# The down projection as one level of Strassen: seven half-size products, their sums on VectorE, weights streamed from DRAM

## The reference, cut to what matters

```python
x = fwht(x * SU_ug) / SCALE
x_up = x @ W_up.T * (Wscale_ug[:INTER] * SCALE)
x_gate = x @ W_gate.T * (Wscale_ug[INTER:] * SCALE)
x = jax.nn.silu(x_gate) * x_up
x = fwht(x * SU_dp) / SCALE
x = x @ W_down.T * (Wscale_dp * SCALE)
```

## Time and profile before

| | us |
|---|---|
| median of 3 runs | 1850.89 (1848.28 to 1851.36) |
| the profiled execution, device time | 1849.29 |
| its span | 1847.2 |
| main work begins on PE | 161.9 |
| block 1 begins on PE | 268.3 |
| last matmul ends | 1841.9 |
| one block, 1 to 14 | 104.9 |

### The profile page before, as it was taken

One profiled execution on the slowest core, in us unless ns is written; L12 is line 12 of the kernel. 1 busy time (PEld: TensorE's weight loads), 2 busy tenths in 40 slices (PEclk: granted clock), 3 DMA queues, 4 the chain that ended last, 5 costly groups with the idle time before them and its releaser, 6 DMA issues.

```text
span 1847.2 us, 37874 instructions
## 1 busy us (share of the span) xinstructions
PE 1794.1 (97%) x13746; PEld 1241.8 (67%) x13746; DVE 1383.8 (75%) x2859; ACT 1224.6 (66%) x2582; POOL 307.7 (17%) x270
## 2 busy tenths in 40 slices
PE   4878999999999999999999999999999999999998
PEld 2336667576766768676766758677666757676675
DVE  6987867869586877858586877958686776958686
ACT  7967848576574848566584847666584857667483
POOL 0000212213030212203021221203021220303021
PEclk9999999999999999999999999999999999999999
DMA  8221223121312223131312322131322213131232
GB/s 326 69 69 49 56 58 81 32 82 38 81 47 62 77 47 76 41 78 41 89 47 58 81 45 76 36 77 47 86 53 58 81 34 75 43 81 47 65 75 58
DMA packets 217573, 125.68 MB, mean 68 GB/s; under 512 B 179662, under 2 KB 180790, under 8 KB 216886
## 3 DMA queue, kind: packets, MB, share of 16 engines
q1 hardware_dynamic: 216870, 122.30, 25.1%
q10 hardware_dynamic: 528, 1.05, 0.2%
HBM read 72.18 MB, written 8.65 MB: 44 GB/s over the span
## 4 chain that ended last, share of the span: by engine, by line
PE 90%; DVE 5%; ACT 1%; DMA 1%; issue 1%; SPq 1%; DVEq 1%; ACTq 0%
PE bank L912 88%; DVE wug L624 1%; DVE wi L666 1%; DMA wi<-n_L_attn_out_proj_w_dram 1%; PE bank L728 1%; PE bank L729 0%; DVE big L509 0%; ACT big L460 0%; DVE wo L675 0%; ACT wi L432 0%; SPq L873 0%; PE bank L717 0%; DVE wd L509 0%; DVE big L510 0%; ACT wi L464 0%
## 5 line engine op out<-in xcount | busy, mean ns | idle before, releaser
L912 PE MATMUL bank<-pair,wug 128*128 128x256 f16 x6144 | 699.8, 273 | 0.0
L912 PEld LDWEIGHTS bank<-pair,wug 128*128 128x128 f16 x6144 | 596.2, 98 | 90.4 <-issue 3.4
L912 PE MATMUL bank<-wd,h 128*128 128x512 f16 x1536 | 360.3, 379 | 0.0
L1185 POOL TENSOR_TENSOR state<-state,dec 128x512 f32<-128x512 f32 x64 | 87.5, 1377 | 1066.3 <-ACT neg L1100 805.7
L912 PEld LDWEIGHTS bank<-wd,h 128*128 128x128 f16 x1536 | 149.2, 98 | 160.4 <-DVE h L1243 0.2
L1232 DVE SCALAR_TENSOR_TENSOR pair<-pair,conv 128x256 f32<-128x256 f32 x384 | 180.2, 514 | 79.0 <-ACT pair L1048 69.1
L912 PE MATMUL bank<-wi,pair 128*128 128x512 f16 (+1 forms) x1152 | 201.6, 330 | 3.1 <-DVEq L1345 3.1
L912 PE MATMUL bank<-pair,wi 128*128 128x256 f16 x1536 | 173.1, 273 | 0.0
L912 PEld LDWEIGHTS bank<-wi,pair 128*128 128x128 f16 x1152 | 101.4, 99 | 98.1 <-issue 3.9
L1114 ACT ACTIVATE Mx<-Mx,cs_own 128x128 f32<-128x128 f32 x512 | 162.2, 388 | 7.6 <-DMA Mx<-cs_rows 7.4
L912 PEld LDWEIGHTS bank<-pair,wi 128*128 128x128 f16 x1536 | 150.0, 98 | 17.0
(11 more groups left out here) (253 smaller groups left out, 2717.0 us busy)
## 6 DMA issues: line engine op xcount, KB each, us to landing
Mx<-cs_rows SPq DMA_DIRECT2D x128, 256.0 KB, 3.6
pair<-in_L_attn_u_dram SPq DMA_DIRECT2D x17, 512.0 KB, 3.6
Mx<-in_L_attn_u_dram SPq DMA_DIRECT2D x16, 512.0 KB, 3.7
out_dram<-Mx SPq DMA_DIRECT2D x16, 512.0 KB, 2.8
big<-in_L_ffn_W_down_dram SPq DMA_DIRECT2D x2, 2048.0 KB, 17.8
wug<-in_L_attn_in_proj_w_dram SPq DMA_DIRECT2D x2, 2048.0 KB, 13.4
pair<-in_L_ffn_W_gate_dram SPq DMA_DIRECT2D x4, 1024.0 KB, 5.3
pair<-in_L_ffn_W_up_dram SPq DMA_DIRECT2D x3, 1024.0 KB, 16.6
```

Source lines behind the costliest of these rows:

```text
L912: ins = nc.tensor.matmul(out, lhsT, rhs, start=first and n == 0, stop=last and n == len(pairs) - 1)
L1185: pool.tensor_tensor(half, half, bcast(dec3[:, 2, c, 8 * hf:8 * hf + 8], HD), ALU.mult).then_inc(state_faded, 1)
```

## The change: what it does, and the diff

The down product of a block is `[256 tokens x 2048] x [2048 x 512]`. The change takes the 16 groups of 128 hidden units in pairs, splits tokens, hidden units and outputs in two, and so has, for each of eight pairs, a product of two 2 x 2 matrices whose entries are 128 x 128 and 128 x 256. Strassen's scheme does it in seven block products instead of eight: steps E0 to E7 take the place of D0 to D15 on PE, 21 matmuls of 256 columns each.

- The left factors: VectorE's new step S makes five sums of the quarters in three instructions (`half_sums`); ScalarE's H and VectorE's L split two plain quarters and five sums into high and low, per pair of groups, in two instructions each (256 and 640 elements).
- The right factors, seven for each pair, are made in the preparation: `part_sums` (ds), high parts (dh, ScalarE), low parts (dl, VectorE), stored to DRAM (`wd_rows`, 917 KB for a pair). In every block SyncE's new steps wl0 to wl7 load them back, into three buffers `ws`; each load waits until the pair three before it has been used.
- The seven results lie in four PSUM banks, so the ring of four serves F, O and all else; F and O are new in the ring. `fin` combines the seven into the output with six dependent instructions, with a drain ahead of each; O0 and O1 are added by VectorE's new steps of that name.
- SyncE and POOL loops are unrolled, small loads in the preparation move from SyncE's queue to ScalarE's, PE no longer waits for the end of the preparation, and all lists of steps are new.

```diff
 PE_STEPS = """
...
+F11 F12 int10 z01 E4 st10 F13 itr10 int11 z10 itr11 F14 z11 F15 E5 O0 st11 E6 E7 O1
...
 DVE_STEPS = """
...
+int11 itr11 lnb ssq1 z10 F14 yl10 z11 S6 lnc yl11 sl10 F15 L6 xl0 vl11 S7 st11 L7 sl11 xl1
...
+wl0 wl1 wl2 bw td0 bd00 bd01 td1 store td2 bd02 bd03 td3 wl3 xin bd10 wl4 bd11 bd12 wl5 bd13 wl6 wl7 yd00 yd01
+res yd10 yd11 xd
...
+RING_READER = {"bc": "dve", "xp": "act", "qk": "dve", "cs": "act", "G": "dve", "F": "dve",
+               "int": "dve", "itr": "dve", "st": "dve", "z": "act", "O": "dve"}
...
+    wd_dram = nc.dram_tensor("wd_rows", [KG, P, 7, 2, HALF], F16, kind="Internal").ap()
...
+            def part_sums(eng, ops, n):
+
+                b, o = part[n % 2], part_sum[n % 2]
+                eng.wait_ge(hw_high, UG_UNITS + 2 * n + 2)
+                if n >= 2:
+                    eng.wait_ge(part_ready, n - 1)
+                ops.tensor_tensor(o[:, 0:2, :], b[:, 0::2, :], b[:, 1::2, :], ALU.add)
+                ops.tensor_tensor(o[:, 2:4, :], b[:, 2:4, :], b[:, 0:2, :], ALU.subtract)
+                ops.tensor_tensor(o[:, 4, :], b[:, 0, :], b[:, 3, :], ALU.add).then_inc(part_summed, 1)
...
+                    elif k == "dh":
...
+                        nc.scalar.activation(part_out[n % 2][:, 0:2, 0, :], part[n % 2][:, 0::3, :], ACT.Copy)
+                        nc.scalar.activation(part_out[n % 2][:, 2:7, 0, :], part_sum[n % 2], ACT.Copy).then_inc(part_high, 1)
...
+                    elif k == "dl":
...
+                        nc.vector.tensor_tensor(o[:, 0:2, 1, :], part[n % 2][:, 0::3, :], o[:, 0:2, 0, :], ALU.subtract)
+                        nc.vector.tensor_tensor(o[:, 2:7, 1, :], part_sum[n % 2], o[:, 2:7, 0, :], ALU.subtract).then_inc(part_ready, 1)
...
+                    elif k == "wl":
+                        g = i * KG + at[0]
...
+                        sp.wait_ge(h_used, g + KG - 2)
+                        sp.dma_start(ws[g % 3][:, :, :, :], wd_dram[at[0]]).then_inc(wd_loaded[g % 3], 16)
...
-                    elif k == "D":
-                        c = number(at)
-                        pe.wait_ge(h_ready, (i + 1) * KF + c + 1)
-                        if c == 0:
+                    elif k == "E":
+                        n = at[0]
+                        g = i * KG + n
+                        pe.wait_ge(h_ready, g + KG + 1)
+                        pe.wait_ge(wd_loaded[g % 3], (g // 3 + 1) * 16)
+                        if n == 0:
                             pe.wait_ge(acc_emptied, i + 1)
-                        for j in range(NT):
-                            ins = products(acc[j][:, :], three(lambda u: h[c % 3][:, u, j * P:(j + 1) * P], lambda u: wd[:, c, u, :]),
-                                           first=c == 0, last=c == KF - 1 and down_closes(j))
+                        a, w = hs[g % 2], ws[g % 3]
+                        for left, right, to in ((5, 3, M7), (2, 1, M5), (3, 0, M2), (4, 2, M6), (6, 6, M1), (1, 4, M4), (0, 5, M3)):
+                            ins = products(acc[:, to, :], three(lambda u: a[:, u, left, :], lambda u: w[:, right, u, :]),
+                                           first=n == 0 and to in (M7, M2, M1, M3), last=n == KG - 1)
                         ins.then_inc(h_used, 1)
...
+        def half_sums(eng, ops, i, n):
...
+            eng.wait_ge(h_whole, (i + 1) * KF + 2 * n + 2)
+            eng.wait_ge(h_ready, (i + 1) * KG + n)
+            ops.tensor_tensor(hsum[:, 0:2, :], x[:, 0:2, :], x[:, 2:4, :], ALU.add)
+            ops.tensor_tensor(hsum[:, 2:4, :], x[:, 1:3, :], x[:, 0::3, :], ALU.subtract)
+            ops.tensor_tensor(hsum[:, 4, :], x[:, 0, :], x[:, 3, :], ALU.add).then_inc(summed, 1)
...
+                    elif k == "S":
+                        dve.drain()
+                        half_sums(dve, nc.vector, i, at[0])
                     elif k == "L":
...
+                        dve.wait_ge(h_high, (i + 1) * KG + n + 1)
+                        nc.vector.tensor_tensor(hs[n % 2][:, 1, 0:2, :], tp[n % 2][:, 0::3, :], hs[n % 2][:, 0, 0:2, :], ALU.subtract)
+                        nc.vector.tensor_tensor(hs[n % 2][:, 1, 2:7, :], hsum[:, :, :], hs[n % 2][:, 0, 2:7, :], ALU.subtract).then_inc(h_ready, 1)
...
+                for terms, to, scale in ((acc[:, M7:M5 + 1, :], quarter[:, 0:2, :], S_OUT), (acc[:, M2:M6 + 1, :], quarter[:, 2:4, :], S_OUT),
+                                         (both(M1), quarter[:, 0::3, :], S_OUT), (both(M3), quarter[:, 1::2, :], S_NEG),
+                                         (both(M4), quarter[:, 0::2, :], S_OUT), (acc[:, M5:M2 + 1, :], quarter[:, 0::3, :], S_NEG)):
+                    dve.drain()
+                    ins = nc.vector.scalar_tensor_tensor(to, terms, scale, to, ALU.mult, ALU.add)
```

More of the change, by code:

```diff
@@ L29 @@
 KF = FF // P
+KG = KF // 2
+HALF = DM // 2
 BC0 = 2 * DI
@@ L55 @@
 PE_STEPS = """
-bc xp0 xp1 F0 qk cs F1 xp2 xp3 F2 F3 F4 G F5 D0 D1 D2 int00 int01 F6 F7 D3 D4 D5 itr00 F8 F9 itr01 D6 st00 F10
-D7 F11 st01 D8 z00 int10 z01 D9 itr10 F12 F13 int11 D10 itr11 st10 F14 D11 z10 z11 F15 D12 O0 D13 D14 st11 D15
-O1
+bc xp0 xp1 cs F0 xp2 F1 qk F2 xp3 F3 F4 F5 F6 F7 G E0 F8 int00 F9 E1 itr00 F10 st00 E2 itr01 int01 E3 z00 st01
+F11 F12 int10 z01 E4 st10 F13 itr10 int11 z10 itr11 F14 z11 F15 E5 O0 st11 E6 E7 O1
 """.split()
 ACT_STEPS = """
-elu xp0 xb0 xp1 qk xb1 cs F0 sv0 kh sv1 th0 F1 th1 xp2 H0 H1 xp3 F2 dr00 F3 xb2 dr01 xb3 dr02 sv2 H2 th2 H3
@@ L65 @@
+mh10 de11 z00 F11 vh10 sh01 dr12 mh11 dr13 F12 de12 yh00 de13 z01 H5 mh12 F13 mh13 yh01 ssq1 vh11 z10 F14 yh10
+z11 sh10 F15 yh11 xh0 H6 H7 sh11 xh1
 """.split()
 DVE_STEPS = """
-bc fin elu cv0 cv1 F0 kl tl0 F1 tl1 L0 L1 qk F2 F3 cv2 cv3 L2 G tl2 L3 F4 tl3 F5 dec00 dec01 dec02 L4 ml00 L5
-ml01 dec03 F6 F7 ml02 int00 L6 vl00 ml03 L7 F8 lna F9 itr00 dec10 int01 st00 L8 itr01 vl01 ml10 L9 sl00 dec11
-st01 ssq0 ml11 dec12 dec13 F10 F11 int10 ml12 L10 z00 L11 vl10 sl01 ml13 F12 itr10 lnb int11 z01 yl00 itr11
@@ L70 @@
-F13 yl01 lnc vl11 ssq1 L12 z10 L13 st10 F14 yl10 z11 L14 xl0 yl11 F15 xl1 L15 st11 sl10 sl11
+O0 O1 bc elu cv0 cv1 tl0 F0 fin F1 tl1 S0 qk cv2 F2 L0 F3 tl2 S1 cv3 L1 kl F4 tl3 F5 S2 F6 G dec00 dec01 F7 L2
+ml00 dec02 ml01 dec03 S3 F8 ml02 int00 vl00 ml03 L3 st00 F9 itr00 S4 F10 int01 itr01 dec10 vl01 lna L4 sl00
+ssq0 st01 ml10 F11 dec11 sl01 S5 z00 vl10 F12 int10 dec12 ml11 st10 dec13 yl00 z01 L5 ml12 itr10 F13 ml13 yl01
+int11 itr11 lnb ssq1 z10 F14 yl10 z11 S6 lnc yl11 sl10 F15 L6 xl0 vl11 S7 st11 L7 sl11 xl1
@@ L903, in bank @@
                 return position(s)
[L905 to L907 removed]
             def products(out, pairs, first=True, last=True):
                 for n, (lhsT, rhs) in enumerate(pairs):
[L912 removed]
+                    ins = nc.tensor.matmul(out, lhsT, rhs, start=first and n == 0, stop=last and n == len(pairs) - 1, skip_group_check=not (first and last))
                 return ins
```

248 lines of the change are left out of this document (153 added, 95 removed).

## The result

The changed kernel takes 2058.9 us (median of four executions, 2057.8 to 2060.1), against 1850.9 for the kernel before (median of three; a fourth execution took 10461 us and is left out): a ratio of 1.113, 95% interval 1.111 to 1.114. The prediction was 1936, range 1888 to 1988: right in direction, and 123 us too low. The profiled execution spans 2058.0 us.

The account below looks back on a forecast made before the run. PE, busy 97%, bounds the kernel, VectorE next; with the change a block would take 109.6 us for 104.9. Span 1847.2 + 15 x 4.7 + 11 + 4 = 1933, predicted time 1936 us, range 1888 to 1988.

Parts of the forecast that it names:

- E7: PE's second to last step of a block: 21 matmuls of 0.109 us, 2.3 us, waiting for VectorE's late split step.
- PE sets this point by some 2.5 us: Block's start to st00: PE done at 49.6 us, VectorE arrives at 47, so PE decides when the second half starts.
- PE's part: PE in a block: 168 down-product matmuls at 109 ns take 18.35 us for 20.75 before; PE alone needs 102.5.
- VectorE's part: VectorE in a block: S, L and fin bring the sum to +16.8 us, busy about 93.7 us, still under PE.
- The crowded half: VectorE from st00 to L7, nearly without gaps: 52.3 us together, from a base of 44.9 us.
- The upper bound of 55 us: VectorE from st00 to L7 at 55 us, drains and POOL's hold dearer: period 112.3, total 1976 us.
- The chain at the end: Block's end: PE's last two steps, 2.3 and 5.2 us, follow VectorE's L7, so 7.5 us behind it.
- The preparation: Before block 0: ScalarE's eight added dh steps, 16.5 us, partly in waiting time; VectorE starts block 0 some 11 us later.
- Block 0: First block: VectorE has no O and no fin there; PE still needs 43 us from cs to st00.
- Rival 3: PE's new waits of 2 to 4 us late in each block lower its clock: 1962 to 1987 us (11%).
- E6: PE's down-product step late in a block; one of four places where PE would wait, 7 us in all.
- Rivals 1, 2 and 4: PE sets time, faster, 1830 (6%); same time, 1847 to 1855 (4%); weight loads hold up the queue, 2011 (7%).

Follow-up runs that it names:

- the run with fills: The changed kernel with GpSimd's products replaced by zero fills of the same tiles, twice for each product: 1934.6 us, period 108.5 us.

## Why the prediction was wrong, point by point

The profiled span of 2058.0 us is 125 over the forecast's 1933: 15 x 6.75 = 101 are in the blocks, 13 in the preparation, 11.5 in block 0; the tail was right. By cause, from the run with fills: the hold adds 7.9 us in each of the 16 blocks, 126 in all; block 0 is 3.6 longer without it; the preparation adds 13; and the rest of the forecast was too dear by 1.1 us a block, 17 in all. The step that failed is when VectorE reaches st00 ("PE sets this point by some 2.5 us"). VectorE's list was priced by rows of a kernel in which VectorE had slack; the hold of GpSimd's reads, which is larger with the added steps, had no term in the sum and stood only in a bound of the other half.

- **PE's part**: right. E's matmuls take 109 ns, and PE waits, 10.8 us in block 2 for 7 forecast.
- **VectorE's part**: the total is near, 95.8 us busy for 93.7 forecast, but by luck: 8.8 of the 95.8 are hold, where the block that the forecast started from held 3.7. With the fills, without the hold, it is 87.9. S, L and fin by themselves cost what was said: undisturbed, S's three instructions stand at 0.34, 0.34 and 0.20 from start to start, and L's at 0.34 and 0.74.
- **"PE sets this point by some 2.5 us"**: this step failed. VectorE starts st00 54.2 us into block 2, not at 47, and PE, done with it at 51.6, is ahead:

```profile
419.84 1.66 PE L975 MATMUL bank<-wi,pair 128*128 128x144 f16 x24
...
430.71 2.79 DVE L1318 SCALAR_TENSOR_TENSOR pair<-pair,conv 128x256 f32<-128x256 f32 x6 [1.12 <-ACT pair L1116]
...
470.65 0.82 PE L975 MATMUL bank<-vw,k 128*128 128x512 f16 x3
```

  Of VectorE's 43.3 us from the second convolution on, 4.3 are hold, and 2.4 waits of over 0.15 us, 1.1 of them at ml00 for ScalarE; the remaining 36.6 stand against 34.1 of the forecast, to which it had added 1.7 for gaps. The step had written that each us of VectorE's being later is added to the period, and 4.6 us were. 3.6 of them are the hold's, for without it VectorE starts st00 at 50.6; that it does so behind PE even then is the step's own error.
- **The crowded half**: 54.8 us in block 2 for 52.3 forecast. 4.5 are hold; before, the same half held 1.5, so the rows that the base came from contained some of it, and without the hold it takes 50.3. The upper bound of 55 us ("the drains and POOL's hold dearer") was right for this term. The range failed because the other half was given no such bound. (The lower bound's terms add up to 1898, not to 1896; nothing hangs on it.)
- **The chain at the end**: right. E7 and O1 take 7.5 us behind L7. That a shorter one would give the 5.2 us of O1 back is not so (2053 us): st11 and PE's own steps from itr11 on stand close behind.
- **The preparation**: 24 us in place of 11, and for another reason. The prediction summed ScalarE's dh. VectorE's sums and low parts, 8 x 3.5 us (0.60 + 0.60 + 0.34 for a pair's sums, 0.60 + 1.40 for its low parts), were left out of the sum; they replace 16 low parts of 0.66, so VectorE has some 18 us more. PE begins the first Hadamard product of a down unit 7.6 us later than before, the last 17.9, the main work 23.9. The runs show that ScalarE alone is not the cost. Nor does PE run bc, xp0 and xp1 ahead, as the prediction had it. Its own wait for the end of the preparation is gone, but bc's place in the ring is freed by VectorE (line 1451) behind VectorE's wait for that end, and both begin at 185.80:

```profile
185.80 3.04 PE L975 MATMUL bank<-wi,pair 128*128 128x144 f16 x24 [9.07 <-DVEq L1451]
```

- **Block 0**: it was given no extra time, on the ground that VectorE has no O and no fin in it. It grew from 106.4 to 117.9, as the others did; with the fills, without the hold, it takes 110.0.
- **Rival 3, the clock**: the clock does fall. PE's waits were to stand ahead of st11, E6 and E7; the long one, 3.41 us, is at itr11, and the clock falls behind it in 14 of blocks 1 to 15 (block 2, columns as in the earlier trace rows):

```profile
508.00:512.00 4.00, 4.00 (x30) 3.11 (x28) 2.78 (x9) 2.01 (x4) 0.00 (x0) 0.66 0.37 70
```

  A granted clock of 0.66 over these 4 us is a mixture of 1.2 and 2.4 GHz; F14 takes 4.07 us there in place of 2.78. But E7 still waits for L7 in 12 of the 15 blocks, so there the loss is taken from PE's slack. In blocks 4, 5 and 6, where E7 does not wait, itr11 to the block's end takes 28.96, 28.80 and 30.00 us, against 28.5 in the shortest blocks (in block 6 the clock falls later, behind a wait of 2.00 us at st11). By that the clock costs some 2.3 us in all, an estimate, where the rival had 26 to 51. The rule from the Trainium skill (TensorE: Matmul & The Clock Gate, section "A second HAM failure mode: psum-queue depth-cycling") was thus right in that the clock falls once in nearly every block; the loss of throughput that it speaks of is small here, where PE is seldom what ends last.
- **Rivals 1, 2 and 4**: not seen. PE waits throughout, the time is 11% longer, and loads of 16 KB change nothing.

The total without the hold, 1934.6 us, lies by the prediction's 1936, but that is partly chance: its period is 1.1 lower than forecast and its preparation 13 us longer.

No version beats the kernel before; of the complete ones with an edit, S on GpSimd is the fastest at 2034 us.

## What to carry to other kernels

When an engine goes from having slack to setting the time, reprice all of its instructions, not only the added ones: whatever was lengthened for free before, here 3.7 to 4.9 us of a block, is now paid, and added instructions of the same kind raise it. Before giving work to VectorE, look which of its instructions have two inputs in SBUF and what GpSimd reads meanwhile. And where a move is costed on one engine, sum the same step on every engine that it touches: the preparation's cost was on VectorE and SyncE, not on the engine that was counted.

## What was not expected of the hardware

- A VectorE instruction with both inputs in SBUF that meets a GpSimd product takes 0.62 us longer in the mean (231 of the 1040 such two-tensor instructions of the changed kernel's main work; the other 809 exceed their shortest tenth by 0.004). The order decides who waits: of the 231, the 43 that start before GpSimd's instruction are not lengthened, and a GpSimd product that waits goes from 1.04 to as much as 1.6 us. VectorE's three-input form (scalar_tensor_tensor) is held as well: in the kernel before, 96 of those with all their tensors in SBUF meet a GpSimd product, and are 0.35 us longer in the mean. Half of GpSimd's 17 us of undisturbed reads in a block of the changed kernel came back as time of VectorE.
- GpSimd's fills of the same tiles, as long in sum, cost VectorE nothing: the 370 such instructions that meet a fill are 0.003 us longer.
- A turn of a tile holds SyncE for 1.2 to 1.3 us to issue, two stores of 896 KB for 0.9 to 1.1 together.
